# Sorted mixture-of-experts rows: weights read from SBUF by a register, token rows as the stationary operand, and one DMA for twenty copies

## The reference, cut to what matters

```python
logits = xt @ Wg                      # 4096 x 8
probs = softmax(logits)
# every expert marks its 512 best tokens; a token goes to the marked expert
# with the highest probability, or without a mark to its own best
tok2exp = ...
weights = probs[token, tok2exp]
for e in range(8):
    gate = where(tok2exp == e, weights, 0.0)
    h = gelu(xt @ W1[e]) @ W2[e]      # W1: 128 x 256, W2: 256 x 128
    out = out + gate[:, None] * h
x = x + out
```

## Time and profile before

| | us |
|---|---|
| median of 3 runs | 782.64 (782.57 to 783.52) |
| the profiled execution, its own time | 784.88 |
| its span in the profile | 783.0 |
| TensorE busy | 678.1 (87%) |
| VectorE busy | 611.3 (78%) |
| ScalarE busy | 469.9 (60%) |
| GpSimd busy | 421.2 (54%) |
| moved by DMA | 60.81 MB |

### The profile page before, as it was taken

How to read it: one execution, slowest core, us unless ns; L and a number is a source line. 1 busy time by engine, 2 the same in 40 slices (tenths; PEclk the granted TensorE clock), 3 DMA queues, 4 the chain that set the end, 5 groups by cost and what they waited for, 6 DMA issues and landing times.

```text
span 783.0 us, 29155 instructions
## 1 busy us (share of the span) xinstructions
PE 678.1 (87%) x9915; PEld 533.0 (68%) x9915; DVE 611.3 (78%) x1435; ACT 469.9 (60%) x1499; POOL 421.2 (54%) x459
## 2 busy tenths in 40 slices
PE   4732999999999999999999975599999949999875
PEld 2422767777777777777777754477777738889764
DVE  6413989899999999999999966678888857779621
ACT  2732777777777777777777833445555444445542
POOL 4740464465455456455463318667777739407365
PEclk9975999999999999999999998789999958999988
DMA  7497434444444444444442003000000000007880
GB/s 167 103 162 180 90 80 87 90 85 96 89 89 96 86 88 96 85 96 88 82 83 62 1 3 107 2 3 4 3 0 0 5 1 1 1 1 227 273 266 25
DMA packets 195181, 60.81 MB, mean 78 GB/s; under 512 B 147556, under 2 KB 193512, under 8 KB 195122
## 3 DMA queue, kind: packets, MB, share of 16 engines
q1 hardware_dynamic: 192000, 55.65, 33.0%
q0 software_dynamic: 1824, 3.96, 1.4%
q10 hardware_dynamic: 1298, 0.40, 0.2%
HBM read 51.58 MB, written 8.83 MB: 77 GB/s over the span
## 4 chain that ended last, share of the span: by engine, by line
PE 48%; SPq 18%; DVE 10%; issue 9%; ACT 8%; POOL 3%; ACTq 1%; DMA 1%; DVEq 0%; POOLq 0%
PE bank L500 22%; PE energy L500 14%; PE bank L503 13%; SPq L531 9%; ACT PR L663 7%; DVE STAT L1545 2%; SPq L537 2%; DVE X L1813 2%; SPq L579 1%; SPq L554 1%; SPq L581 1%; POOL SX L954 1%; SPq L576 1%; POOL TQ L946 1%; DMA MK<-in_mask_BxSxS_ik 1%
## 5 line engine op out<-in xcount | busy, mean ns | idle before, releaser
L663 ACT ACTIVATE PR<-energy,STAT 128x256 f32<-128x256 f32 x512 | 234.4, 483 | 117.1 <-DVE STAT L1545 117.1
L1545 DVE TENSOR_REDUCE STAT<-energy 128x512 f32 (+1 forms) x256 | 164.1, 684 | 28.0 <-PE energy L500 27.8
L503 PE MATMUL bank<-ident,PR 128*128 128x128 f32 x1024 | 152.6, 283 | 30.5 <-DVE PT L1562 25.7
L1562 DVE COPY PT<-bank 128x512 f32<-128x512 f32 x256 | 161.6, 670 | 1.3 <-PE bank L503 1.3
L503 PEld LDWEIGHTS bank<-ident,PR 128*128 128x128 f32 x1024 | 110.0, 142 | 61.3 <-issue 49.7
L851 POOL TENSOR_TENSOR QB<-QT,headmask 128x512 f32<-128x512 f32 x32 | 33.3, 1040 | 193.0 <-DMA MK<-in_mask_BxSxS_ik 131.8
L663 ACT ACTIVATION_READ_ACCUMULATOR PR<-energy,STAT (+1 forms) x512 | 110.4, 216 | 0.0
L858 POOL TENSOR_SCALAR MZ<-MK 128x512 bf16<-128x512 int32 x64 | 94.1, 1487 | 5.9 <-DMA MK<-in_mask_BxSxS_ik 5.9
L500 PEld LDWEIGHTS bank<-wv_s,CT 128*128 128x128 f32 x512 | 67.8, 194 | 31.8 <-issue 31.7
L500 PE MATMUL bank<-PT,VT 128*32 128x128 f32 x2048 | 70.1, 278 | 0.1
L500 PE MATMUL bank<-wv_s,CT 128*128 128x128 f32 x512 | 68.4, 277 | 0.4 <-DVE OC L1554 0.4
(11 more groups left out here) (284 smaller groups left out, 1277.9 us busy)
## 6 DMA issues: line engine op xcount, KB each, us to landing
CX<-in_ctx SPq DMA_DIRECT2D x512, 32.0 KB, 2.6
MK<-in_mask_BxSxS_ik SPq DMA_DIRECT2D x128, 128.0 KB
rows_in<-fill SPq DMA_DIRECT2D x1, 3483.0 KB, 20.9
X<-in_x SPq DMA_DIRECT2D x4, 512.0 KB, 7.6
VLT<-v_last SPq DMA_DIRECT2D x4, 512.0 KB, 9.5
QT<-in_L_ffn_W SPq DMA_DIRECT2D x16, 128.0 KB, 3.5
OT<-in_L_ffn_W SPq DMA_DIRECT2D x16, 128.0 KB
PAY<-rows_in SPq DMA_DIRECT2D x2, 903.0 KB, 8.0
```

The costliest lines, as they stand in the source:

```text
L503: return nc.tensor.transpose(o, i, ident[0:n, 0:n])
L663: nc.scalar.activation(PR[:, b, g, :], EB[:, g, e * KEYS:(e + 1) * KEYS], ACT.Exp, bias=STAT[:, bass.ds(t, 1), b, 1, g:g + 1].rearrange("p ...
L1545: V.tensor_reduce(STAT[:, bass.ds(t, 1), b:b + 2, 1, g:g + 1].rearrange("p a b g -> p (a b g)"), EB[:, g, :].rearrange("p (e k) -> p e k", ...
L1562: V.tensor_copy(PT[:, k % 2, e, 2 * half:2 * half + 2, :].rearrange("p g k -> p (g k)"), psum[1 if e else 7]).then_inc(ev_t, 1)
```

## The change

- **Weights.** SyncE no longer loads expert weights. TensorE loads the expert numbers into its own registers, four before each expansion from unit 17 on (`load_experts`), and its slot matmuls read `w1_s` and `w2_s`, which lie in SBUF for the dense units, at an address computed from the register.
- **The hidden product.** The transposed rows `XST` become the stationary operand and `W1` the moving one: one matmul of 256 columns in place of two of 128. The result is [token, feature], so after the gelu TensorE transposes it by two transposes (`turn_hidden`) and VectorE copies the 128 x 256 result to SBUF (`evac_hidden`, into `HTS`) before `expand_rows`. A pass of the slot loop now has four TensorE steps, of slots t, t-1, t-2 and t-3.
- **The original rows in `PAY`.** One DMA from SyncE, issued when self-attention has ended (`a_x2`), copies the 20 tiles of `X` in place of GpSimd's twenty copies. GpSimd waits for it (`pay_ld`) before the scatters.
- **The rest of group 1** (`input_rest(1, 1)`) moves from behind the 20 normalisations to behind the tenth.
- **Held additions.** VectorE adds the first 18 kept units before the slots, and the last six (`HELD`) in quarters, one instruction in each slot.

```diff
+        FIRST_LOAD = 17
+        HELD = 6
+        HTS = QT[:, 0:3 * F].rearrange("p (t f) -> p t f", t=3)
@@ sync
+            sp.wait_ge(a_x2, NT)
+            sp.dma_start(PAY[:, :, P:2 * P], X[:, DENSE:NT, :]).then_inc(pay_ld, 16)
...
-            for t in range(16):
-                load_weights(t)
             sp.wait_ge(sent, 16 * SORTED)
             for k, (a, z) in enumerate(zip(GROUPS, GROUPS[1:])):
...
-            for t in range(16, SLOTS):
-                load_weights(t)
@@ scalar, gelu_rows
-                wait_reuse(act, s_y, t - 2)
+                wait_reuse(act, s_turned, t - 2)
@@ gpsimd
             for t in range(DENSE, NT):
                 normalised(PAY[:, t - DENSE, 0:P], t).then_inc(r_pn, 1)
-                nc.gpsimd.tensor_copy(PAY[:, t - DENSE, P:2 * P], X[:, t, :]).then_inc(pay_x, 1)
+                if t == DENSE + 9:
+                    input_rest(1, 1)
...
-            input_rest(1, 1)
             input_rest(2, 0)
-            pool.wait_ge(pay_x, SORTED + 1)
+            pool.wait_ge(pay_x, 1)
+            pool.wait_ge(pay_ld, 16)
@@ tensor
+            def load_experts(n):
+                if not own:
+                    pe.wait_ge(s_own, 1)
+                for t in range(len(own), min(len(own) + n, SLOTS)):
+                    own.append(pe.value_load(OWN[0:1, t:t + 1], min_val=0, max_val=E - 1))
...
+                if u >= FIRST_LOAD:
+                    load_experts(4)
                 expand(u // E, u % E, between)
@@ tensor, hidden_rows
-                for j in range(FC):
-                    last = mm(psum[t % 4][:, j * P:(j + 1) * P],
-                              expert_w1(t)[:, j * P:(j + 1) * P], XST[:, t % 3, :])
+                last = mm(psum[t % 4][:, 0:F], XST[:, t % 3, :],
+                          w1_s[:, bass.ds(own[t], 1), :].rearrange("p a f -> p (a f)"))
@@ tensor
+            def turn_hidden(t):
+                pe.wait_ge(s_g, t + 1)
+                for j in range(FC):
+                    last = tr(psum[t % 4][:, F + j * P:F + (j + 1) * P], HST[:, t % 3, j * P:(j + 1) * P])
+                last.then_inc(s_turned, 1)
@@ tensor, expand_rows
-                pe.wait_ge(s_g, t + 1)
+                pe.wait_ge(s_ht, t + 1)
...
-                    last = mm(psum[4 + t % 2][:, 0:P], HST[:, t % 3, j * P:(j + 1) * P],
-                              expert_w2(t)[:, j * P:(j + 1) * P],
+                    last = mm(psum[4 + t % 2][:, 0:P], HTS[:, t % 3, j * P:(j + 1) * P],
+                              w2_s[:, bass.ds(own[t], 1), j, :].rearrange("p a c -> p (a c)"),
@@ vector
+            def evac_hidden(t):
+                dve.wait_ge(s_turned, t + 1)
+                wait_reuse(dve, s_y, t - 2)
+                V.tensor_copy(HTS[:, t % 3, :], psum[t % 4][:, F:2 * F]).then_inc(s_ht, 1)
...
-            for i in range(LATE):
-                for e in range(E):
-                    add_kept(i, e)
-            for t in range(SLOTS):
-                add_rows(t)
+            for u in range(LATE * E - HELD):
+                add_kept(u // E, u % E)
+            for t in range(SLOTS + 1):
+                if t < SLOTS:
+                    evac_hidden(t)
+                if t:
+                    add_rows(t - 1)
+                u = LATE * E - HELD + t // 4
+                if u < LATE * E:
+                    add_kept(u // E, u % E, [t % 4])
```

More of the change, by code:

```diff
@@ L440, in perceiver_block @@
         sent = sem("sent")
-        ld_w = [sem(f"ld_w{k}") for k in range(len(WAVES) - 1)]
+        pay_ld = sem("pay_ld")
+        s_turned = sem("s_turned")
+        s_ht = sem("s_ht")
         ld_row = [sem(f"ld_row{k}") for k in range(len(GROUPS) - 1)]
@@ L1398, in _ @@
             router_step(1)
+            own = []
+            def load_experts(n):
[3 more added lines that the diff above has]
+                    own.append(pe.value_load(OWN[0:1, t:t + 1], min_val=0, max_val=E - 1))
             for u in range(LATE * E):
@@ L1433, in expand_rows @@
                 for j in range(FC):
-                    last = mm(psum[4 + t % 2][:, 0:P], HST[:, t % 3, j * P:(j + 1) * P],
-                              expert_w2(t)[:, j * P:(j + 1) * P],
+                    last = mm(psum[4 + t % 2][:, 0:P], HTS[:, t % 3, j * P:(j + 1) * P],
+                              w2_s[:, bass.ds(own[t], 1), j, :].rearrange("p a c -> p (a c)"),
                               start=(j == 0), stop=(j == FC - 1))
                 last.then_inc(s_y, 1)
-            for t in range(SLOTS + 2):
+            for t in range(SLOTS + 3):
                 if t < SLOTS:
@@ L1443, in _ @@
                     hidden_rows(t - 1)
-                if t >= 2:
-                    expand_rows(t - 2)
+                if 0 <= t - 2 < SLOTS:
+                    turn_hidden(t - 2)
+                if t >= 3:
+                    expand_rows(t - 3)
         @block.vector
@@ L1808, in _, with add @@
             link(gates(DENSE, NT))
-            def add(i, e, outputs, done):
-                for t in range(4):
+            def add(i, e, outputs, done, quarters=range(4)):
+                for t in quarters:
                     xi = X[:, bass.ds(i * 4 + t, 1), :].rearrange("p a c -> p (a c)")
@@ L1849, in _, with add_kept @@
             dve.wait_ge(t_done, 1)
-            def add_kept(i, e):
+            def add_kept(i, e, quarters=range(4)):
                 dve.wait_ge(f_keep, i * E + e + 1)
                 if e:
-                    dve.wait_ge(f_late, 4 * (i * E + e))
-                add(i, e, KEPT[i][e], f_late)
+                    dve.wait_ge(f_late, 4 * (i * E + e) - 3 + quarters[-1])
+                add(i, e, KEPT[i][e], f_late, quarters)
+            def evac_hidden(t):
+                dve.wait_ge(s_turned, t + 1)
+                wait_reuse(dve, s_y, t - 2)
+                V.tensor_copy(HTS[:, t % 3, :], psum[t % 4][:, F:2 * F]).then_inc(s_ht, 1)
             def add_rows(t):
```

30 lines of the change are left out of this document (2 added, 28 removed).

## The result

Five runs of the changed kernel have a median of **778.62 us** (776.63 to 782.96), five of the kernel before 782.64 (781.42 to 786.51). The medians lie 4.0 us apart, where 5.74 were forecast. The recorded ratio of the two kernels is 0.9938, with a 95% interval of 0.9915 to 0.9961, which is 4.9 us (3.1 to 6.7) of 782.64. The profiled execution of the changed kernel has a time of 781.64 us and a span of 779.7; that of before had 784.88, so the two traces lie 3.24 us apart.

The account below looks back on a forecast made before the run. Bounds: a late router step, late row loads and slot 15's weight wait, with GpSimd's output DMAs pacing the slots. Terms -1.07 - 2.04 + 0.42 - 3.05 = -5.74 us, from 782.64 to 776.9 us; range 775.3 to 781.2.

Parts of the forecast that it names:

- the likeliest case: Whole kernel: faster by more than 0.2% (1.6 us), chance 0.83, against within 0.2% at 0.06 and slower at 0.11.
- (a): Router before the dense units: moving the rest of group 1 ends VectorE's 1.39 us operation and TensorE's wait, -1.07 us.
- (b): After self-attention: twenty GpSimd copies become one SyncE DMA with 65 us of cover, cost 0.
- (c): Turn from dense units to slots: without SyncE's 54 weight loads, rows land early and the transpose gap goes, -2.04 us.
- (d): First transpose to first output DMA: one more pipeline stage, +1.00, less the 0.58 wait for second rows, +0.42 us.
- (e): Slots: GpSimd's 1.29 us per slot stays the limit, now unbroken by the weight wait, -3.05 us.
- the rival of a longer slot period: Slots: register addresses and waits raise the period to 1.40 us, 2.9 us given back, 779.8 us; chance 0.16.
- (f): Dense units 17 to 23: 27 value loads on TensorE's sequencer, 0.50 us each, hidden behind queued matmuls, 0 us.
- The partly exposed rival: Units 17 to 23: value loads of 0.85 us each outrun the lead, costing 5.3 us, result 782.2 us; chance 0.08.
- (g): Slots: six held VectorE additions run inside the slots, the others ending near 729 us before them, 0 us.
- The rival that they block output DMAs: Slots: each of 24 GpSimd output DMAs waits for one addition, 7.2 us, result 784.1 us; chance 0.03.
- The signs to look for: Trace: no gap before a transpose near 733.7, L1758 short, 27 unbroken output DMAs, last near 772.1, clock 1.00, no SyncE weight loads.

Follow-up runs that it names:

- experiment 2: Changed kernel with the twenty copies on GpSimd again instead of one DMA, the rest of group 1 staying behind the tenth normalisation: 778.12 us, ratio to before 0.9949.
- experiment 1: Changed kernel with the rest of group 1 back behind the twentieth normalisation, the copies staying one DMA: 780.31 us, ratio to before 0.9973.
- experiment 4: Changed kernel with value loads begun one unit earlier, three before units 16 to 20, four before 21 to 23: 779.59 us, ratio to before 0.9959.
- experiment 3: Changed kernel without value loads, slot t using expert t modulo 8 at a fixed address: 776.89 us, ratio to before 0.9921.
- experiment 5: Kernel before with only GpSimd's half: copies by DMA, rest of group 1 behind the tenth normalisation, weights still loaded by SyncE: 780.30 us, ratio 0.9981.
- experiment 10: Changed kernel with value loads begun at unit 15, at most four a unit, none between units 22 and 23: 778.98 us, ratio to before 0.9931.
- experiment 11: Changed kernel with GpSimd's order of before, copies on GpSimd and rest of group 1 behind the twentieth normalisation: 779.38 us, ratio to before 0.9934.
- experiment 6: Changed kernel with SyncE issuing the 54 weight loads again into places nothing reads, TensorE's value loads staying: 778.94 us, ratio to before 0.9955.
- experiment 8: Experiment 4 with two slots' transposes before the last half of the last unit, their eviction ahead of ScalarE's last held copy: 776.94 us, ratio to before 0.9922.
- experiment 12: Experiments 10 and 8 together on the changed kernel, the transposes one quarter later: 776.14 us, ratio to before 0.9893.
- experiment 9: Changed kernel with no held additions (HELD = 0), each standing behind its own unit: 778.18 us, ratio to before 0.993.
- experiment 7: Changed kernel with all 27 value loads behind the last dense unit, before the first slot's transpose: 794.52 us, ratio to before 1.0148.

## Why the prediction was right and where it was not

**The sign, the size within the range and the likeliest case were right; the point was 1.7 us too low** (776.9 against 778.62, and 779.1 against 781.64 for the profiled execution). By its steps:

(a) *The rest of group 1, -1.07.* Right as a mechanism and a size as long as the copies stand on GpSimd: -1.12 by experiment 2 at an equal clock rise. It is not a term of its own: with the copies gone as well the late rest fell where it cost nothing (experiments 1 and 4, 55.92 both), so only the pair (a) and (b) has a price. In the trace of the changed kernel it does not show, because the clock rose 3.6 us later. Experiments 1 and 4 (55.92 at 4.7) and 3, 5 and the changed kernel (56.89, 56.96, 57.00 at 8.3 to 8.4) put 1.0 to 1.1 us on that. It is not the change's: experiments 1 and 2 and 4 have the early rise, and 5 has the late one with weights still loaded.

(b) *The copies as a DMA, 0.* The step named only GpSimd's own time, where the 65 us of cover are real. It left out what the copies did to VectorE's router steps: some are a tenth of a microsecond longer, 0.40 in all between experiments 1 or 4 and 2. Together (a) and (b) give -1.5 at equal clock (57.44 to 55.92), 1.8 by experiments 10 and 11.

(c) *Weight loads gone from SyncE, -2.04.* Right, as far as the runs reach: the row loads are issued 2.41 us earlier, the transpose has no gap, and without value loads it comes 33.27 - 31.09 = 2.18 us earlier after the slot cast (experiment 3). Experiment 6 does not price the queue, since its 1.3 us are slower number loads on TensorE. An estimate: rows issued 29.31 us after the cast, as there, and usable 2.83 us later would come at 32.1, 1.0 us after TensorE is free in experiment 3.

(d) *One stage more, +0.42.* It was +0.79, and the stretch 5.17 to 5.31 us instead of 4.94 in all traces of the new slots with a clock that stayed up. The step counted TensorE's added passes but not ScalarE's queue: its last held copy of 0.60 us stands ahead of the first row's eviction, and the first slot's matmul waits 0.64 to 0.73 us. Experiments 8 and 12, which move that copy and the transposes, have no such wait and end 0.48 and 0.52 us earlier than 4 and 10. The landing of the second rows, on which the forecast put 0.58 us, was not the limit.

(e) *Slot cost, -3.05.* Right: -2.90, since a period is 1.296 us and not 1.29. TensorE took 1.21 for a slot (transposes of rows start at 741.85, 743.06 and 744.27), below it, and the rival of a longer slot period fell in all twelve traces with the new slots.

(f) *Value loads hidden, 0.* **This is the step that failed**, and the term that was mis-sized: they cost 1.0 to 1.5 us. The form of the working was right and the price of a load was the error: SyncE's 0.50 us, and so 2.85 us of sequencer work in a unit of 3.17. TensorE's loads for units 17, 18, 19 and 22 of the changed kernel:

```profile
L1375 PEldq TENSOR_LOAD <-OWN x4: 300/306/756, 712.4 to 714.8; - x4
L1375 PEldq TENSOR_LOAD <-OWN x4: 295/299/307, 716.1 to 718.0; - x4
L1375 PEldq TENSOR_LOAD <-OWN x4: 296/301/307, 719.3 to 721.3; - x4
L1375 PEldq TENSOR_LOAD <-OWN x4: 293/295/309, 729.0 to 730.9; - x4
```

Within a unit they start about 0.64 us apart, and from unit to unit (729.0 - 716.1)/4 = 3.2 us: 4 x 0.64, and 0.65 for all else that the sequencer has to issue. That is the pace of the units in this trace (3.20 to 3.26), over 3.17, so TensorE's sequencer sets it. The first four, one of them 0.76 us long, take 712.4 to 715.5, more than the 2.7 us of lead, so unit 17 comes 0.44 us late, and at 3.2 us a unit the lead is never filled again. The last three, between units 22 and 23 with no hidden matmuls beside them, cost 0.36. The partly exposed rival had the mechanism, but from 0.85 us a load. That this cost and the clock's later rise did not take more of the forecast is in part luck: the 0.4 us that (b) had not counted stand against them. (Its 16 ns for an instruction, which it calls an upper bound, is 3.69 us / 229 = 16.1.)

(g) *Held additions, 0.* Right within 0.2 us (experiment 9). The rival that they block output DMAs fell: those took 0.98 us (1.06 in two of 27) with one addition per slot beside them in the first 24, as the earlier trace rows had without. The Trainium skill (SBUF, "SBUF: two separate sides") makes a lock of such a pair; for a two-input VectorE operation against GpSimd's indirect DMA the trace does not agree, while for one against GpSimd's two-input L966 it does in the length of the wait (experiment 11): VectorE's operation ends with GpSimd's, though by the profile's starts it began first, at 669.42 against 669.91.

The sum with the measured terms: -1.5 (a, b) + 1.1 (clock) - 1.17 (c with f) + 0.79 (d) - 2.90 (e) + 0.44 (ahead of the dense layer) = -3.24, which the traces' landmarks have as -3.28. Without the two that are not the change's it is -4.8, and the timed medians say -4.0 (from -6.7 to -3.1 by the interval).

The signs to look for were named beforehand: L1758 short and the router's wait gone (seen), 27 output DMAs in a row (seen, the last at 774.60 and not 772.1), clock 1.00 through the slots (seen), and of those named as wrong, units from 17 on longer than 3.17 us (seen, though what idle time there is the profile puts down to ScalarE and not to issue).

## What to carry to other kernels

Price an instruction on the queue it moves to: a load of an expert number has its own cost on TensorE's sequencer, and the margin of a hidden chain (0.3 us of 3.17 here) has to be larger than the doubt about each of its terms times their number. Look at how far the sequencer is ahead at the place of the new instructions and not only in the mean over the stage, and put them where the queue behind them is longest. A change that takes work off an engine with slack can still pay on another, through the operations that it stretches; and when a kernel's own runs spread by 4 us, compare stretches between landmarks with the same clock, not totals.

## What the runs showed that was not expected

- A value load on TensorE takes about 0.64 us from its start to the next one's, 0.67 on average in the row of 27 of experiment 7, where the forecast had 0.50 from SyncE's rows; the first in a row takes up to 0.76 for its TENSOR_LOAD alone.
- The identical loads cost 1.01 us in one trace and 1.42 to 1.51 in four others (experiments 1, 2, 9 and 11). The difference is in the loads themselves: from the first to the last start they take 20.6 us in the changed kernel (712.4 to 733.0) and 21.0 to 21.1 in the four, in which a few in the middle take up to 0.53 us in place of 0.30. With no lead left, TensorE's units are late by as much. Why single loads are slow is open. Experiment 1, all and those from 714.8 to 718.2:

```profile
L1374 PEldq TENSOR_LOAD <-OWN x27: 294/302/716, 707.8 to 728.9; - x27
L1374 PEldq TENSOR_LOAD <-OWN x5: 295/332/451, 714.8 to 718.2; - x5
```

- The clock's rise in the first dense units comes at about 3.5, 4.7 or 8.3 us after their first matmul in executions of like kernels, worth up to 1.6 us (55.43 in experiment 10 against 57.00), the largest part of what differs ahead of the slot cast between traces with the same work on GpSimd. What decides it was not tried.
- One two-input operation of VectorE on 128x1 took 1.79 us beside GpSimd's 128x512 one.
